# A decoder layer on one core: the last three steps of its attention in an order of their own

## The chip, the core and the metric

The kernel runs on one core of a Trainium2 chip. The number that counts is the device time of one execution in microseconds (us); the median of three runs is given. The engines are PE (matrix products and transposes), ACT, DVE and POOL (elementwise work), and SP, which here only issues DMA transfers. Each takes its instructions in the order of its own program; between engines they wait on semaphores.

## The reference

Sixteen sequences of 256 positions and 256 features pass through three parts, each with its residual added and a layer norm behind it:

```python
x = _layernorm(x + _L0_attn_ref(x, ...))            # gated mixer: projection, convolution of 4, scan, gate
x = _layernorm(x + _L0_xattn_ref(x, ctx, ctx, ...))  # cross attention, 16 heads of 16
x = _layernorm(x + _L0_ffn_ref(x, ...))              # 8 experts, one for each token
# the feed-forward part
probs = softmax(t @ Wr); idx = argmax(probs); pmax = max(probs)
pos = sum(cumsum(onehot, axis=0) * onehot, axis=-1) - 1   # place in the expert, over all 4096 tokens in order
kept = pos < 640
out = where(kept, expert_idx(t), t) * where(kept, pmax, 1)
```

The place of a token in its expert counts all tokens before it. The experts thus can't start before the last sequence has been counted.

## The kernel before

It has three blocks, with a barrier of all engines between them: `mixer_in`, `attend` and `experts`.

`attend` is a software pipeline over sequences, written once as a function `step(n, p)` for each engine. In step n, sequence n gets its keys and queries, n-1 its score maxima, n-2 and n-3 its exponentials and weighted sums, n-3 its output projection, residual and second norm, n-4 its router, counts and the scatter to `rows_dram`. `on(n, lag)` says whether sequence n-lag exists, and `run` (line 473) goes through steps -1 to 19. From step 17 on only the three last sequences are left, called X (13), Y (14) and Z (15) here. A step is laid out by 16 slots h, so what stands where is fixed by these slots, not by what is ready.

The prediction speaks of these pieces:

- PE: `scores_t` (line 756) writes a pair of heads' scores to `ps_a`, which has room for one such pair. `weigh` (766) sums the values of four heads, `sums_by_query` (782) turns the sums, `turn` (720) transposes, `project_out` (792) is the output projection, `router` (801) and `count` (809) give the logits and the running counts. All but the first two write one PSUM bank, `ps_e`; its sibling `ps_d` serves the projections of earlier sequences and has no work after step 16.
- ACT: the exponential of each pair (line 946), read from `ps_a`; copies of turned tiles to SBUF (891, 933, 951).
- DVE: the division of the sums (1063, 1064), the residual (1088), the norm that gives `pay` (999), and a chain of small operations on the router's logits: top, index, one-hot `hot` (1028), `slot0` (1030), place, `dest` (1056).
- POOL: the power -1/2 for the second norm (675) and for a third one (641), the doubled norm `twice` (645), and the scatter of `pay`, two indirect DMAs for a sequence (656).
- SP: loads. In step 16 it issues the first expert's weights, 2 MB (588, 589); after the last scatter has landed, the first expert's rows in three pieces (602).

`count` writes its counts into the columns of `ps_e` that `sums_by_query` would overwrite, so line 785 makes the sums of sequence j wait until the counts of j-1 have been read (`place_done`).

`experts` takes expert e: PE forms the hidden layer in eight parts f (line 1202, three products each of split operands). After parts 4, 5 and 6 it transposes a piece of the rows of expert e+1 (`turn_rows`, 1181, with the matmuls of line 1189), and after part 7 begins the product down (1216, 1222). SP's step (1158) loads for expert e its two weight matrices and then its rows; for e = 1 the second matrix waits for `w2_lo` of expert 0, POOL's operation of line 1357.

## Time and profile before

| | |
|---|---|
| time, median of 3 runs | 922.13 us (921.59 to 923.24) |
| the profiled execution | 924.1 us, of which the span 922.3 us |
| PE busy | 791.4 us, 86% of the span |
| DVE busy | 601.1 us, 65% |
| ACT busy | 400.9 us, 43% |
| POOL busy | 357.4 us, 39% |
| mean granted clock of PE | 0.93 of full speed |

The busy shares are averages over three blocks with different limits. Read in stretches, PE is busy 9 tenths and more of nearly every slice from 690 us to the end, and between 600 and 660 us, where attention runs out, it is not. Rows of the timeline give the start and the length of an instruction in microseconds; `xN` says how many were merged into the row, and what stands in brackets is how long the engine had been idle before it and what ended that.

### The profile page before, as it was taken

What the parts mean: (1) busy time and instruction counts of PE and PEld (TensorE: products, weight loads), DVE (VectorE), ACT (ScalarE), POOL (GpSimd) and SP (SyncE); (2) the same over time, 40 slices, a digit from 0 to 9 for tenths busy, and PEclk for the clock granted to TensorE, in tenths of its full rate; (3) what the DMA queues carried; (4) which work ended last, traced back from release to release, by engine and by line L of the source; (5) the groups of instructions that cost most, each with busy time, mean ns of one, the idle gap of its engine ahead of it and who ended that gap; (6) DMA issues with size and microseconds to landing.
All of it is one profiled execution on the core that took longest, in us unless ns stands there. A gap on an engine that the chain in (4) does not pass through costs nothing. (4 is left out here: it accounts for less than half of the span.)

```text
span 922.3 us, 16301 instructions
## 1 busy us (share of the span) xinstructions
PE 791.4 (86%) x5613; PEld 618.2 (67%) x5613; DVE 601.1 (65%) x1450; ACT 400.9 (43%) x639; POOL 357.4 (39%) x290
## 2 busy tenths in 40 slices
PE   4999873588998999999999998876389999999992
PEld 3777652355666666676666666544389999999992
DVE  4888856455578767777877777643346667666652
ACT  4666630114565555555555546451242334423320
POOL 0333334422254544544454453223312544245422
PEclk9999997778999999999999999895599999999997
DMA  4115701534543454554445344400223423343100
GB/s 127 47 32 153 211 1 52 147 109 139 144 153 113 136 150 127 157 162 129 130 133 165 119 135 139 149 22 22 96 75 120 133 99 92 110 133 125 42 29 18
DMA packets 75943, 100.87 MB, mean 109 GB/s; under 512 B 10993, under 2 KB 63386, under 8 KB 75888
## 3 DMA queue, kind: packets, MB, share of 16 engines
q1 hardware_dynamic: 72432, 92.03, 33.6%
q0 software_dynamic: 3456, 8.13, 2.5%
q8 instruction: 32, 0.52, 0.2%
q14 instruction: 23, 0.19, 0.1%
HBM read 65.47 MB, written 35.74 MB: 110 GB/s over the span
## 5 line engine op out<-in xcount | busy, mean ns | idle before, releaser
L992 DVE TENSOR_REDUCE nmax<-ps_m 128x4 f32<-128x1024 f32 x128 | 156.6, 1224 | 60.9 <-PE ps_m L752 49.9
L946 ACT ACTIVATE pt<-ps_a 128x1024 f32<-128x1024 f32 x128 | 131.4, 1026 | 98.3 <-PE ps_a L762 74.7
L1269 ACT ACTIVATE hid<-ps_h 128x640 fp32r<-128x640 f32 x64 | 45.1, 705 | 145.9 <-PE ps_h L1202 145.9
L1202 PE MATMUL ps_h<-xt,w_hi 128*128 128x320 f32 x512 | 101.8, 322 | 1.0 <-DVE xt L1284 1.0
L752 PE MATMUL ps_m<-kst,qst 48*128 48x256 f32 x512 | 67.4, 342 | 25.4 <-DVE nmax L992 21.7
L1319 DVE SCALAR_TENSOR_TENSOR hid<-ps_h,hid 128x640 fp32r<-128x640 f32 x64 | 52.8, 825 | 50.0 <-ACT hid L1269 49.7
L1369 POOL DMA_INDIRECT out_rows<-gated,token x40 | 49.9, 1246 | 88.5 <-issue 88.5
L1202 PEld LDWEIGHTS ps_h<-xt,w_hi 128*128 128x128 f32 x512 | 80.8, 193 | 4.2 <-DVE hid L1319 2.2
L629 POOL TENSOR_TENSOR half<-kq,half 128x512 fp32r<-128x512 f32 x32 | 41.7, 1302 | 105.3 <-ACT half L884 105.3
L752 PEld LDWEIGHTS ps_m<-kst,qst 48*128 48x128 f32 x512 | 40.3, 194 | 62.5 <-DVE nmax L992 32.1
L1216 PE MATMUL ps_y<-w,hid 128*128 128x512 f32 x320 | 80.1, 392 | 0.0
L166 POOL TENSOR_TENSOR gated<-xh,sgate 128x512 f32<-128x512 f32 x32 | 42.3, 1322 | 88.1 <-ACT xh L259 88.1
L354 DVE SCALAR_TENSOR_TENSOR conv<-ps_xh,taps,conv 128x510 f32<-128x510 f32 (+2 forms) x96 | 71.7, 747 | 3.4
L777 PE MATMUL ps_o<-pt,vals 128*32 128x256 f32 x1024 | 72.1, 401 | 0.0
L715 PE MATMUL ps_d<-w_out_sb,y 128*128 128x256 f32 x256 | 62.2, 388 | 11.2 <-DVE y L1040 9.8
L1216 PEld LDWEIGHTS ps_y<-w,hid 128*128 128x128 f32 x320 | 57.7, 189 | 10.3
L656 POOL DMA_INDIRECT rows_dram<-pay,dest x32 | 33.1, 1036 | 75.8 <-DVE dest L1056 66.8
L715 PEld LDWEIGHTS ps_d<-w_out_sb,y 128*128 128x128 f32 x256 | 47.3, 194 | 18.6 <-issue 11.6
L1202 PE MATMUL ps_h<-xt,w_lo 128*128 128x320 f32 x256 | 59.4, 314 | 0.0
L762 PE MATMUL ps_a<-qst,kst 49*128 49x256 f32 x512 | 53.7, 288 | 0.6 <-ACT pt L946 0.4
L1357 POOL TENSOR_TENSOR w<-gated,w 128x2048 fp32r<-128x2048 f32 x8 | 39.0, 4880 | 28.1 <-ACT w L1258 28.1
L695 PE MATMUL ps_d<-ctx,w_k_sb 128*128 128x256 f32 x128 | 39.2, 435 | 10.7 <-DMA ctx<-in_ctx_t 9.6
(170 smaller groups left out, 1596.1 us busy)
## 6 DMA issues: line engine op xcount, KB each, us to landing
halves_dram<-half SPq DMA_DIRECT2D x64, 256.0 KB, 2.5
gated<-in_w SPq DMA_DIRECT2D x16, 1024.0 KB, 5.2
kst<-halves_dram SPq DMA_DIRECT2D x64, 128.0 KB, 2.7
qst<-halves_dram SPq DMA_DIRECT2D x64, 128.0 KB, 2.9
rows_dram<-blank SPq DMA_DIRECT2D x1, 5160.0 KB, 18.9
gated<-rows_dram SPq DMA_DIRECT2D x7, 645.0 KB, 4.2
x_raw<-in_x_t SPq DMA_DIRECT2D x8, 512.0 KB, 3.7
xres<-in_x SPq DMA_DIRECT2D x16, 256.0 KB, 3.4
```

The lines of the kernel that those rows point to most:

```text
L354: op = nc.vector.scalar_tensor_tensor(out[:, :, late:S], ps[:, :, 0:S - late], taps[:, m, k:k + 1], out[:, :, late:S], ALU.mult, ALU.add)
L715: mm = pe.matmul(ps_d[:, t * D:(t + 1) * D], y[:, m, t * P:(t + 1) * P], w["out"][:, m, :], start=(m == 0), stop=(m == MH - 1), skip_group ...
L752: mm = pe.matmul(ps_m[:, side, t, :], qst[base:base + MR, p, k, t * P:(t + 1) * P], kst[base:base + MR, p, k, :], start=True, stop=True, s ...
L762: mm = pe.matmul(ps_a[:, side, t, :], kst[base:base + MR + 1, p, k, t * P:(t + 1) * P], qst[base:base + MR + 1, p, k, :], start=True, stop ...
L777: mm = pe.matmul(ps_o[VW * i:VW * (i + 1), g, :], vals[:, p, t, h, :], pt[:, h // 2 % 4, h % 2, t, :], start=(t == 0), stop=(t == KT - 1), ...
L946: nc.scalar.activation(pt[:, k % 4].rearrange("p s t q -> p (s t q)"), ps_a[:].rearrange("p s t q -> p (s t q)"), ACT.Exp).then_inc(s["exp ...
L992: nc.vector.tensor_reduce(nmax[:, q, :, :, h // 2].rearrange("p t s -> p s t"), ps_m[:], AX.X, ALU.max, negate=True).then_inc(s["max_done" ...
L1202: mm = pe.matmul(ps_h[:, f % 2, c2, 0:HC], w1[a][:, p, k, f * P:(f + 1) * P], xt[:, b, p, k, c2 * HC:(c2 + 1) * HC], start=(n == 0 and k = ...
L1216: pe.matmul(ps_y[:, (p + t) % 2, 0:2 * D], hid[:, HI, f, t * P:(t + 1) * P], w2[:, p, f].rearrange("p a d -> p (a d)"), start=(f == 0), st ...
L1269: nc.scalar.activation(hid[:, HI, f, :].rearrange("p (c n) -> p c n", c=2), ps_h[:, f % 2, :, 0:HC], ACT.Relu).then_inc(s["hid_hi"], 1)
L1319: nc.vector.scalar_tensor_tensor(hid[:, LO, f, :].rearrange("p (c n) -> p c n", c=2), ps_h[:, f % 2, :, 0:HC], 0.0, hid[:, HI, f, :].rearr ...
L1369: nc.gpsimd.indirect_dma_start(out=dram["out"], out_offset=bass.IndirectOffsetOnAxis(ap=token[:, p, t:t + 1], axis=0), in_=new[:, p, t, :] ...
```

## The change

Steps 17, 18 and 19 are no longer run through `step` on PE, ACT and DVE. The pieces of `step` become functions with the same instructions, and the three engines call them in lists written out. SP and POOL keep their steps. Four things differ in what runs:

1. The lists order some pieces otherwise than the slots did.
2. Z's turned sums, its transpose and its output projection go to `ps_d` (function `bank`), without the wait for Y's counts.
3. On POOL, from step 17 on, the power for the second norm stands ahead of the scatter; on SP the first expert's weights are issued in step 17, behind the transfer of the row of maxima, and no longer in step 16.
4. In `experts`, SP issues the rows of expert 1 at the start of the block, ahead of that expert's weights.

```diff
-    def run(eng, step):
+    def run(eng, step, end=B + 4):
...
+    X, Y, Z = B - 3, B - 2, B - 1
+
+    def bank(j):
+
+        return ps_d if isinstance(j, int) and j == Z else ps_e
...
-                if isinstance(n, int) and n == B:
+                if isinstance(n, int) and n == B + 1:
                     sp.wait_ge(s["y_done"], B)
                     sp.dma_start(c["w1_raw"], ...
...
+            def rstd2(j):
+                pool.wait_ge(s["var2_ready"], j + 1)
+                nc.gpsimd.tensor_tensor(ve2[:], ve2[:], power[:], ALU.pow).then_inc(s["rstd2"], 1)
...
+                late = isinstance(n, int) and n > B
+                if late and on(n, 3):
+                    rstd2(n - 3)
                 if on(n, 4):
...
-                if on(n, 3):
-                    j = n - 3
...
+                if on(n, 3) and not late:
+                    rstd2(n - 3)
...
                     pe.wait_ge(s["oraw_hi"], j + 1)
-                    need(pe, s["place_done"], j)
+                    if bank(j) is ps_e:
+                        need(pe, s["place_done"], j)
...
-            run(pe, step)
+            run(pe, step, B + 1)
+
+            scores_t(Y, 0, NP - 2)
+            maxima_rows(Z, 1)
...
+            scores_t(Z, 1, 7)
+            turn_x2(Y, 0)
+            weigh(Z, 1, 3)
+            router(Y)
+            sums_by_query(Z, 0)
+            sums_by_query(Z, 1)
+            count(Y)
+            turn_normed(Z)
+            project_out(Z, 0)
...
-            run(dve, step)
+            run(dve, step, B + 1)
...
+            top_of(Y)
+            hot_of(ry, Y)
+            normed(oz, Z, 0)
+            normed(oz, Z, 1)
+            picked(Y)
+            placed(Y)
+            slotted(Y, 0)
+            sent_to(Y, 0)
+            residual2(Z)
...
+            def load_rows(e, p):
+                need(sp, s["res_done"], (e - 1) * TS)
+                need(sp, s["token_done"], e - 1)
+                sp.dma_start(rows[:, p], dram["rows"][bass.ds(e * CAP, CAP), :]...
...
                 if first:
-                    return
-                need(sp, s["res_done"], (e - 1) * TS)
-                need(sp, s["token_done"], e - 1)
-                sp.dma_start(rows[:, p], dram["rows"][bass.ds(e * CAP, CAP), :]...
+                    load_rows(1, 1)
+                elif not isinstance(e, int) or e > 1:
+                    load_rows(e, p)
```

On ACT one piece moves: the copy of Y's last sums stands ahead of Z's first exponential. On DVE, besides what the diff shows, the destination of X moves ahead of the division of Y's sums.

PE in step 17, before. `pay` is X's normed input to the router, `x2t` its transpose, the `ps_a` rows are Z's scores 0 and 1, `ps_o` is the last part of Y's weighted sums:

```order
L723 MATMUL ps_e<-eye,pay 128x128 [waits m_out,x2_done]
L723 MATMUL ps_e<-eye,pay 128x128 x3
L762 MATMUL ps_a<-qst,kst 128x256 [waits exp_done,m_in]
L762 MATMUL ps_a<-qst,kst 128x256 x3
L777 MATMUL ps_o<-pt,vals 32x256 [waits exp_done]
L777 MATMUL ps_o<-pt,vals 32x256 x7
L805 MATMUL ps_e<-w_r_sb,x2t 128x8 [waits x2t_out]
L805 MATMUL ps_e<-w_r_sb,x2t 128x8 x3
L762 MATMUL ps_a<-qst,kst 128x256 [waits exp_done]
L762 MATMUL ps_a<-qst,kst 128x256 x3
L815 MATMUL ps_e<-hot,tri 128x8 [waits carry_ready,hot_ready]
```

And in the changed kernel:

```order
L734 MATMUL ps_e<-eye,pay 128x128 [waits m_out,x2_done]
L734 MATMUL ps_e<-eye,pay 128x128 x3
L788 MATMUL ps_o<-pt,vals 32x256 [waits exp_done]
L788 MATMUL ps_o<-pt,vals 32x256 x7
L817 MATMUL ps_e<-w_r_sb,x2t 128x8 [waits x2t_out]
L817 MATMUL ps_e<-w_r_sb,x2t 128x8 x3
L773 MATMUL ps_a<-qst,kst 128x256 [waits exp_done,m_in]
L773 MATMUL ps_a<-qst,kst 128x256 x3
L773 MATMUL ps_a<-qst,kst 128x256 [waits exp_done]
L773 MATMUL ps_a<-qst,kst 128x256 x3
L827 MATMUL ps_e<-hot,tri 128x8 [waits carry_ready,hot_ready]
```

Z's first scores moved from ahead of Y's weighted sums and X's router to behind both.

PE in step 18, before: Y's router, Y's counts, then Z's sums and their transpose:

```order
L805 MATMUL ps_e<-w_r_sb,x2t 128x8 [waits x2t_out]
L805 MATMUL ps_e<-w_r_sb,x2t 128x8 x3
L815 MATMUL ps_e<-hot,tri 128x8 [waits carry_ready,hot_ready]
L818 MATMUL ps_e<-carry,ones_b 128x8
L815 MATMUL ps_e<-hot,tri 128x8
L817 MATMUL ps_e<-hot,ones_b 128x8
L818 MATMUL ps_e<-carry,ones_b 128x8
L789 MATMUL ps_e<-eye,oraw 128x128 [waits place_done,oraw_hi]
L789 MATMUL ps_e<-eye,oraw 128x128 x3
L789 MATMUL ps_e<-eye,oraw 128x128 [waits on_done]
L789 MATMUL ps_e<-eye,oraw 128x128 x3
L723 MATMUL ps_e<-eye,onrm 128x128 [waits on_done]
```

And in the changed kernel:

```order
L817 MATMUL ps_e<-w_r_sb,x2t 128x8 [waits x2t_out]
L817 MATMUL ps_e<-w_r_sb,x2t 128x8 x3
L801 MATMUL ps_d<-eye,oraw 128x128 [waits oraw_hi]
L801 MATMUL ps_d<-eye,oraw 128x128 x3
L801 MATMUL ps_d<-eye,oraw 128x128 [waits on_done]
L801 MATMUL ps_d<-eye,oraw 128x128 x3
L827 MATMUL ps_e<-hot,tri 128x8 [waits carry_ready,hot_ready]
L830 MATMUL ps_e<-carry,ones_b 128x8
L827 MATMUL ps_e<-hot,tri 128x8
L829 MATMUL ps_e<-hot,ones_b 128x8
L830 MATMUL ps_e<-carry,ones_b 128x8
L734 MATMUL ps_d<-eye,onrm 128x128 [waits on_done]
```

Z's two groups of sums now stand ahead of Y's counts, in the other bank, and only the first matmul of the counts waits for `hot_ready`.

POOL in steps 18 and 19, before: `twice` and scatter of Y, the power of Z's second norm, then the power of Z's third norm:

```order
L645 TENSOR_SCALAR twice<-pay,mv,ve 128x256 [waits rstd3,setup_pe]
L645 TENSOR_SCALAR twice<-pay,mv,ve 128x256
L656 DMA rows_dram<-pay,dest 5120x258 [waits pay_ready,dest_ready,setup_pe]
L656 DMA rows_dram<-pay,dest 5120x258
L675 TENSOR_TENSOR ve<-ve,power 128x2 [waits var2_ready]
L641 TENSOR_TENSOR ve<-ve,power 128x2 [waits out_sent1,var3_ready]
L645 TENSOR_SCALAR twice<-pay,mv,ve 128x256 [waits rstd3,setup_pe]
```

And in the changed kernel:

```order
L655 TENSOR_SCALAR twice<-pay,mv,ve 128x256 [waits rstd3,setup_pe]
L655 TENSOR_SCALAR twice<-pay,mv,ve 128x256
L639 TENSOR_TENSOR ve<-ve,power 128x2 [waits var2_ready]
L669 DMA rows_dram<-pay,dest 5120x258 [waits pay_ready,dest_ready,setup_pe]
L669 DMA rows_dram<-pay,dest 5120x258
L651 TENSOR_TENSOR ve<-ve,power 128x2 [waits out_sent1,var3_ready]
L655 TENSOR_SCALAR twice<-pay,mv,ve 128x256 [waits rstd3,setup_pe]
```

The scatter of Y moved behind the power of Z's second norm, so it stands directly ahead of the third norm's work for Z.

## Rows read from the trace of the kernel before

**Rows 1.** Stretches: length, busy time of PE, PEld, DVE, ACT, POOL, granted clock, DMA.
```profile
605.50:608.90 3.40, 1.88 (x23) 1.48 (x26) 2.01 (x16) 2.03 (x8) 2.10 (x2) 1.00 0.11 35
608.90:612.30 3.40, 3.40 (x24) 1.65 (x16) 0.93 (x7) 0.96 (x1) 0.00 (x0) 0.50 0.14 47
...
684.50:700.00 15.50, 15.50 (x92) 13.67 (x91) 9.81 (x18) 4.31 (x3) 6.62 (x1) 1.00 0.37 122
```

**Rows 2.** Timeline, PE, step 17: start us, us, then the instruction and the idle time before.
```profile
602.93 0.65 PE L723 MATMUL ps_e<-eye,pay 128*128 128x128 f32 x4 [1.03 <-DVE pay L999]
603.64 0.50 PE L762 MATMUL ps_a<-qst,kst 49*128 49x256 f32 x4
604.07 1.07 PE L777 MATMUL ps_o<-pt,vals 128*32 128x256 f32 x16
605.07 1.06 PE L805 MATMUL ps_e<-w_r_sb,x2t 128*128 128x8 f32 x8
606.06 0.51 PE L762 MATMUL ps_a<-qst,kst 49*128 49x256 f32 x4
...
608.29 0.51 PE L762 MATMUL ps_a<-qst,kst 49*128 49x256 f32 x4
...
611.52 0.80 PE L762 MATMUL ps_a<-qst,kst 49*128 49x256 f32 x4
...
613.44 0.50 PE L762 MATMUL ps_a<-qst,kst 49*128 49x256 f32 x4 [0.38 <-ACT pt L946]
```

**Rows 3.** Timeline, ACT, step 17: the exponentials of scores 0 and 3 of Z.
```profile
604.18 1.02 ACT L946 ACTIVATE pt<-ps_a 128x1024 f32<-128x1024 f32 x1
...
612.36 1.02 ACT L946 ACTIVATE pt<-ps_a 128x1024 f32<-128x1024 f32 x1 [2.50 <-PE ps_a L762]
```

**Rows 4.** Timeline, PE, step 18: the router of Y and the sums of Z.
```profile
624.35 1.88 PE L805 MATMUL ps_e<-w_r_sb,x2t 128*128 128x8 f32 x8
...
628.78 1.09 PE L789 MATMUL ps_e<-eye,oraw 128*128 128x128 f32 x4 [0.50 <-DVE carry L1035]
630.68 1.11 PE L789 MATMUL ps_e<-eye,oraw 128*128 128x128 f32 x4 [0.81 <-DVE onrm L1064]
632.60 1.12 PE L723 MATMUL ps_e<-eye,onrm 128*128 128x128 f32 x4 [0.81 <-DVE onrm L1064]
```

**Rows 5.** Timeline, DVE, step 18 and the last destination.
```profile
627.83 0.16 DVE L1030 TENSOR_SCALAR slot<-expert 128x2 f32<-128x2 f32 x1
...
629.90 0.26 DVE L1063 RECIPROCAL rec<-ps_e 128x16 f32<-128x16 f32 x1 [0.80 <-PE ps_e L789]
...
648.39 0.16 DVE L1056 TENSOR_TENSOR dest<-slot,over 128x2 int32<-128x2 f32 x1
```

**Rows 6.** Timeline, POOL, steps 18 and 19.
```profile
640.33 0.73 POOL L675 TENSOR_TENSOR ve<-ve,power 128x2 f32<-128x2 f32 x1 [6.41 <-DVE ve L1094]
643.25 0.70 POOL L641 TENSOR_TENSOR ve<-ve,power 128x2 f32<-128x2 f32 x1 [2.19 <-DVE ve L1009]
644.12 2.43 POOL L645 TENSOR_SCALAR twice<-pay,mv,ve 128x256 f32<-128x256 f32 x2 [0.18 <-POOL ve L641]
649.41 1.09 POOL L656 DMA_INDIRECT rows_dram<-pay,dest  x1 [2.87 <-DVE dest L1056]
650.81 0.97 POOL L656 DMA_INDIRECT rows_dram<-pay,dest  x1 [0.30 <-issue]
```

**Rows 7.** Timeline, SP: the load of expert 1's rows.
```profile
669.47 0.57 SPq L1174 DMA_DIRECT2D gated<-rows_dram  x1
```

**Rows 8.** Timeline, PE, expert 0: rows of expert 1 turned, first product down.
```profile
676.60 0.66 PE L1189 MATMUL ps_t<-eye,gated 128*128 128x128 f32 x4 [2.60 <-DMA gated<-rows_dram]
...
684.58 2.00 PE L1216 MATMUL ps_y<-w,hid 128*128 128x512 f32 x8
```

**Rows 9.** Timeline, PE, the same two places one expert later.
```profile
707.74 0.60 PE L1189 MATMUL ps_t<-eye,gated 128*128 128x128 f32 x4
...
714.12 2.00 PE L1216 MATMUL ps_y<-w,hid 128*128 128x512 f32 x8
```

More of the change, by code:

```diff
@@ L479, in run @@
             step(i * 2 + FIRST + 1, (FIRST + 1) % 2)
-        for n in range(LAST + 1, B + 4):
+        for n in range(LAST + 1, end):
             step(n, n % 2)
+    X, Y, Z = B - 3, B - 2, B - 1
+    def bank(j):
+        return ps_d if isinstance(j, int) and j == Z else ps_e
     def on(n, lag):
@@ L788, in sums_by_query @@
                 for g in range(4):
[L789 removed]
+                    mm = pe.transpose(bank(j)[:, g * P:(g + 1) * P], oraw[:, g, t * P:(t + 1) * P], eye[:])
                 mm.then_inc(s["ot_mm"], 1)
@@ L917, in step @@
                     if h == 7 and on(n, 4):
[L918 to L924 removed]
+                        gate_sum(n - 4)
                     if h == 2 and on(n, 0):
@@ L981, in mean_var, with x2_of @@
                 chain.done(op)
+            def x2_of(i, p):
+                dve.wait_ge(s["rstd2"], i + 1)
+                need(dve, sent[p], use(i, 32, p) - 32)
+                need(dve, s["out_ready"], i - 1)
+                for t in range(KT):
+                    op = nc.vector.tensor_scalar(pay[:, p, t, 0:D], c["r2"][:, t, :], mv2[:, t, 0:1],
+                                                 ve2[:, t:t + 1], ALU.subtract, ALU.mult)
+                op.then_inc(s["x2_done"], 1)
+                nc.vector.tensor_copy(pay[:, p, :, D], c["tokens"][:, bass.ds(i * KT, KT)])
@@ new lines, in hot_of @@
+            def hot_of(rc, i):
+                dve.wait_ge(s["vo_row"], 1)
+                dve.wait_ge(s["top_out"], i + 1)
+                for t in range(KT):
+                    op = nc.vector.max_index(where[:, t, :], top[:, t, :], lg[:, t, :])
+                rc.done(op)
+                rc.done(nc.vector.tensor_copy(expert[:], where[:, :, 0]))
+                for t in range(KT):
+                    op = nc.vector.tensor_scalar(hot[:, t, :], c["kinds"][:], expert[:, t:t + 1], None, ALU.is_equal)
+                op.then_inc(s["hot_ready"], 1)
+                rc.done(nc.vector.tensor_scalar(slot0[:], expert[:], float(CAP), -1.0, ALU.mult, ALU.add))
@@ new lines, in normed @@
+            def normed(oc, j, t):
+                dve.wait_ge(s["ot_mm"], 2 * j + t + 1)
+                if t == 0:
+                    need(dve, s["ont_mm"], j)
+                o4 = bank(j)[:].rearrange("p (h w) -> p h w", w=VW)
+                oc.done(nc.vector.reciprocal(rec[:], o4[:, :, HD]))
+                nc.vector.tensor_tensor(onrm[:, t].rearrange("p (h d) -> p h d", d=HD), o4[:, :, 0:HD],
+                                        rec[:, :, None].to_broadcast([P, NH, HD]), ALU.mult
+                                        ).then_inc(s["on_done"], 1)
@@ L1015, in step @@
[L1015 to L1030 removed]
+                        top_of(n - 4)
```

279 lines of the change are left out of this document (180 added, 99 removed).

## The prediction

> **What bounds the kernel now.** I first read the page's slices: PE has 9 tenths and more in nearly all of them from 690 us to the end, at the full granted clock, as the stretch 684.5 to 700 shows (15.50 busy of 15.50) [rows 1]. So what starts the experts' dense part earlier by some microseconds ends the kernel earlier by as much. Then I read the stretches of 600 to 685 us, where the slices thin out, and for each of them the timelines of PE, DVE, ACT and POOL side by side. The reader is to see two kinds of loss there. In the end of attention no engine is full: three sequences pass one by one through a chain PE, DVE, PE, ACT, and each piece waits for the one before. In expert 0, PE waits 2.60 us for a DMA, the rows of expert 1 [rows 8], and runs slowly behind it. The changed stretches are these and no others, so the sum is made up of a part for the experts, a part for step 18 and a part for step 17.
>
> **The experts: rows of expert 1 loaded first.** In the kernel before, SP issues them at 669.47 [rows 7], behind the second weight matrix, and PE gets them at 676.60, after 2.60 us of idleness [rows 8]. The issue now comes with the start of the block. The same transfer takes 7.1 us there, from 669.47 to about 676.6, beside the weights; begun some 13 us earlier it has landed before the hidden layer begins, whatever it meets. So the wait goes: 2.60 us. PE then also goes on without the slow stretch behind the wait. From the first turned piece to the start of the product down it takes 684.58 - 676.60 = 7.98 us in expert 0 [rows 8], and 714.12 - 707.74 = 6.38 us one expert later, with the same instructions and no wait before them [rows 9]. That is 1.60 us more. Sum: 4.20 us. What could be late next is POOL's split of expert 0's second matrix, which the product down needs. The issue at 669.47 stood behind the wait for it, so it is done by then [rows 7], 11 us before PE would now come to it (684.58 - 4.20 = 680.4). From below, if PE stayed at the lower clock behind the turned rows all the same, only 2.60 is left; from above, nothing in the rows gives more than 4.2.
>
> **Step 18: Z's sums in the other bank.** Before, the chain after Y's router is: DVE's top, index and one-hot, PE's counts, DVE's reading of them, and only then Z's first sums at 628.78, released by DVE's `carry` [rows 4]. Now the sums stand directly behind the router and need 1.1 us there. The router begins at 624.35 and takes 1.88, so the sums end at about 627.3, beside DVE's chain, which ends with `slot0` at 627.83 + 0.16 = 627.99 [rows 5]. DVE can begin the division at about 628.05 where it began at 629.90 [rows 5]: 1.85 us earlier. The rest keeps its distances: second sums 0.78 after the first reciprocal (630.68 - 629.90), the transpose 1.92 after these (632.60 - 630.68) [rows 4, 5]. Y's counts stand between the second sums and this transpose on PE; they are five matmuls of 8 columns and lie inside the 0.81 us for which PE waits there anyway [rows 4]. Their readers on DVE lie between the division and Z's residual, inside a wait of several microseconds for the projection. So step 18 gives 1.85 us. If the sums had to wait for anything else of that length, it would give nothing; and more than 1.85 it can't give, as DVE's own chain then ends last.
>
> **POOL's new order.** Y's scatter, two indirect DMAs, stands now between the power of Z's second norm and the third norm of Z. The power ends at 640.33 + 0.73 = 641.06, and the third norm's began at 643.25 [rows 6]. In the rows of Z the scatter starts 0.86 us after the destination is ready (648.39 + 0.16 to 649.41) and takes 2.37 (to 650.81 + 0.97) [rows 5, 6]: 3.2 us together, so POOL is free at 644.3, 1.0 us later than it is wanted. The doubled norm behind it then ends at about 647.6 and not at 646.55 (644.12 + 2.43), while the destination of Z is ready at 648.55 (all in the old clock, from which 1.85 is to be taken). Hidden, with 0.9 us to spare. X's scatter waits now for the power of Y's second norm; the next writer of its buffer is Z's normed input, which comes behind the whole of Y's chain. So this order costs nothing.
>
> **Step 17: an order that is later at first.** Z's first scores stood at 603.64, behind the transpose of X at 602.93 [rows 2]. Now Y's weighted sums and X's router are ahead of them; the sums follow about 0.6 behind the start of that transpose, which is 0.65 long, at 603.52. The weighted sums take 1.00 of issue and the router 0.99 (604.07 to 605.07 to 606.06) [rows 2]; so Z's scores 0 start at 605.51, 1.87 us later. Then the chain of one score buffer runs: exponential 0.54 after the scores start, 1.02 long, next scores 0.06 behind it, 1.62 for each pair [rows 2, 3] (604.18 - 603.64; 613.44 - 612.36). Scores 1 come at 607.13 (606.06 before), scores 2 at 608.75 (608.29 before): 0.46 us late. Most of the delay is made up, because scores 1 waited behind the router before, and X's counts, which held scores 2, are ready 0.5 us earlier.
>
> What follows hangs on the clock. In 605.5 to 608.9 PE was busy 1.88 of 3.40 us, so idle for 1.5 in all, and in the 3.4 us behind this it ran at 0.50 of its clock, the lower of its two levels, 1.2 GHz [rows 1]: scores 3 came 3.23 us after scores 2 (611.52 - 608.29), and their exponential 0.84 after them [rows 2, 3]. At full clock the same pieces need 2.02 us (0.43 from 603.64 to 604.07, 1.00, and 0.6 for turned sums as for the transpose), and the exponential 0.54. The new order leaves PE yet less to do between 605.5 and 608.9 (three sets of scores and the counts, about 1.4 us), so I take it that the clock falls again: scores 3 and all behind them 0.46 us late. At full clock they would be 0.46 - 1.21 - 0.30 = 1.05 early. In the other direction, if the lower clock comes one stretch sooner, the first two sets of scores each lose 0.30 more: 1.06 late. I take 0.45 late, the case nearest to the row, and keep -1.05 and +1.06.
>
> The Trainium skill (TensorE: Matmul & The Clock Gate, "What's actually happening") gives the lower clock as the state behind an idle stretch. By that rule the new order, whose gaps are near 1.2 us (605.51 + 0.4 to 607.13), would keep the full clock, and the sum would be 1.5 us better. The row does not bear it out: the clock fell behind a stretch that was more than half busy.
>
> **The other edits** are put at nothing. The first expert's weights go from step 16 to 17, where the long chains of three sequences lie between them and their use; SP has them behind the small transfers that Z's scores need. What they crowded in step 16 can only come sooner, and I count no gain for it. The copy that moves on ACT goes into time in which ACT would wait for Z's later scores, and X's destination has only the scatter behind it, which waits longer now anyway.
>
> **Sum against the profiled execution:** 924.1 - 4.20 - 1.85 + 0.45 = 918.5 us (the span from 922.3 to 916.7). The profiled execution is 2.0 us above the median of the runs, 922.13; against that the same 5.6 us give **916.5 us**.
>
> **Rivals.**
> - A, the forecast: 5.6 us less, 916.5. Its own range, with step 17 up to 1.06 late and the expert part between 2.6 and 4.2, is 916.1 (step 17 on time) to 918.7.
> - B, the clock holds in step 17: 4.20 + 1.85 + 1.05 = 7.1 less, 915.0. For it: the 1.5 us of idleness come in smaller pieces. Against it: less work in the stretch. It is also what the rule of the Trainium skill gives.
> - C, the end of attention gives nothing: Y's scatter on POOL holds the third norm and thereby Z's scatter, which is the last event that the experts wait for. Its spare time is 0.9 us by the rows; if an indirect DMA takes 2 us more behind another one's descriptors, or the wait for scatters that went out late comes last, the 1.85 is gone: 4.20 less, with step 17's 0.45 on top or not, 917.9 to 918.4. For it: POOL does one thing after another, so a moved scatter holds all behind it. Against: each of these DMAs in the rows takes 1.1 us or less.
> - D, the wait in expert 0 is only exchanged, for the weights' split or the clock: 1.40 less, 920.7. For it: 7.1 us for 645 KB, beside the weights, shows that the transfers crowd. Against: 11 us of spare time.
> - E, slower than before: the clock stays at its lower level through the first expert's hidden layer, because the tail before it keeps PE even less busy. Three parts of it take 6.38 us at the upper level [rows 9], 2.1 each; at the lower one four parts would take 8.5 more. 5.6 less and 8.5 more is 2.9 more than before, 925.0. It decides from the point where more than 5.6 us of work that now runs at the upper level runs at the lower. Against it: the fall of step 17 ended with PE fully busy for 3.4 us [rows 1]; scores 4, at 613.44, are 0.50 long again, scores 3 were 0.80 [rows 2].
>
> The Trainium skill (PSUM — Partial Sum Buffer, "Engine vs sequencer instructions") has the queue of GpSimd as strictly first in, first out. This is C's ground; by the rule alone Z's third norm is late by 1.0 us, which the trace's spare time covers.
>
> **How the numbers follow.** A 0.45, B 0.22, C 0.15, D 0.09, E 0.03; 0.06 for what I don't see, half of it faster. A measurement of this kernel can tell 0.2%, 1.84 us, from no change. A, B and C are beyond that: 0.82, with a part of D and of the rest 0.88 for faster; 0.08 for within; 0.04 for slower. The range takes A, B and C whole and leaves D and E out: from B less the 0.9 by which the runs shown differ from their median, 914.1, to the far end of C with as much again, 919.4 when rounded up.
>
> **What would show it.** The timeline of PE: no idle time ahead of the turned rows of expert 1, and about 6.4 us from them to the product down. DVE's first reciprocal of Z directly behind Y's `slot0`. The granted clock of the stretch behind Z's scores 2: 0.5 says A, 1.0 says B. On POOL, Z's scatter 0.9 us after the destination is ready; a longer distance says C. The forecast is wrong if Z's destination comes less than 0.7 us or more than 3.5 us earlier than 648.39 [rows 5], or if PE idles elsewhere in expert 0.

## The result, and the profile after

| | before | after |
|---|---|---|
| time, median of 8 runs | 920.1 us (916.85 to 923.24) | 916.78 us (914.5 to 918.61) |
| the profiled execution | 924.1 us, span 922.3 us | 917.73 us, span 915.9 us |
| PE busy | 791.4 us | 791.2 us |
| mean granted clock of PE | 0.93 | 0.93 |

The changed kernel takes 0.9953 of the time of the one before (95% interval 0.9936 to 0.997), which is 4.3 us less (2.8 to 5.9). The two medians by themselves lie 3.3 us apart; differences of times below are read from the ratio and its interval unless medians are named. The forecast was 5.6 us less, 0.9939 as a ratio, inside the interval. The forecast time, 916.5 us, is 0.3 us from the median of 916.78, but that closeness is luck: it was counted down from 922.13 us, the median of three runs, and eight runs have their median at 920.1 us.

The two profiled executions differ by 6.4 us of span. Cut at instructions that both have, PE's timelines give this (us; each piece runs from its name to the next):

| from the start of | before | after | difference |
|---|---|---|---|
| the span, to X's transpose | 602.93 | 599.83 | -3.10 |
| X's transpose | 18.98 | 21.43 | +2.45 |
| Y's transpose | 2.44 | 2.85 | +0.41 |
| Y's router | 8.25 | 5.76 | -2.49 |
| the transpose of Z's normed sums, to the hidden layer of expert 0 | 30.44 | 30.45 | +0.01 |
| the hidden layer, to the first turned piece of expert 1 | 13.56 | 11.49 | -2.07 |
| the turned piece, to the product down | 7.98 | 6.38 | -1.60 |
| the product down, to the end | 237.72 | 237.71 | -0.01 |

"Step 17 took" means below the second of these pieces, from X's transpose to Y's. The first line lies in code whose order the change doesn't touch; what it is, is told further down. The rest sums to -3.3 us. Of these the last three pieces, the experts, give 3.68, and the four before them, the end of attention from X's transpose on, came out 0.38 us longer (60.49 for 60.11). So in these two traces the whole gain is that of the experts. PE's rows of the changed kernel show the experts first. These are the first row of the hidden layer, the turned piece and the product down, in the form of [rows 8]: start us, us, then the instruction.

```profile
660.32 1.41 PE L1377 MATMUL ps_h<-xt,w_hi 128*128 128x320 f32 x4 [1.01 <-DVE xt L1459]
...
671.81 0.60 PE L1364 MATMUL ps_t<-eye,gated 128*128 128x128 f32 x4
...
678.19 2.00 PE L1391 MATMUL ps_y<-w,hid 128*128 128x512 f32 x8
```

The turned piece has no bracket behind it, so PE did not wait: the 2.60 us of idleness of [rows 8] are gone. From it to the product down 6.38 us pass, to the hundredth what [rows 9] had one expert later. SP's row of the same kernel has the load at the start of the block, issued 18.2 us before PE takes the rows (before: 7.1 us, from 669.47 in [rows 7] to 676.60 in [rows 8]):

```profile
653.65 0.37 SPq L1332 DMA_DIRECT2D gated<-rows_dram  x1
```

PE in step 18, from Y's router to the projection of Z, answers to [rows 4]:

```profile
624.11 1.37 PE L817 MATMUL ps_e<-w_r_sb,x2t 128*128 128x8 f32 x8
625.33 0.63 PE L801 MATMUL ps_d<-eye,oraw 128*128 128x128 f32 x4
628.05 1.01 PE L801 MATMUL ps_d<-eye,oraw 128*128 128x128 f32 x4 [2.09 <-DVE onrm L1151]
628.86 0.21 PE L827 MATMUL ps_e<-hot,tri 128*128 128x8 bf16 x1
...
629.87 1.12 PE L734 MATMUL ps_d<-eye,onrm 128*128 128x128 f32 x4 [0.70 <-DVE onrm L1151]
```

Z's first sums stand at once behind the router, and were done well before DVE could take them. DVE, in the form of [rows 5], goes from `slot0` to the first reciprocal without a wait, then waits for the second sums; the last row is Z's destination:

```profile
627.09 0.16 DVE L1120 TENSOR_SCALAR slot<-expert 128x2 f32<-128x2 f32 x1
627.28 0.26 DVE L1150 RECIPROCAL rec<-ps_d 128x16 f32<-128x16 f32 x1
...
629.10 0.26 DVE L1150 RECIPROCAL rec<-ps_d 128x16 f32<-128x16 f32 x1 [1.10 <-PE ps_d L801]
...
645.67 0.16 DVE L1143 TENSOR_TENSOR dest<-slot,over 128x2 int32<-128x2 f32 x1
```

POOL, in the form of [rows 6]:

```profile
637.46 0.72 POOL L639 TENSOR_TENSOR ve<-ve,power 128x2 f32<-128x2 f32 x1 [11.16 <-DVE ve L1165]
638.35 1.10 POOL L669 DMA_INDIRECT rows_dram<-pay,dest  x1 [0.18 <-issue]
639.76 0.98 POOL L669 DMA_INDIRECT rows_dram<-pay,dest  x1 [0.30 <-issue]
640.73 0.77 POOL L651 TENSOR_TENSOR ve<-ve,power 128x2 f32<-128x2 f32 x1
641.67 2.43 POOL L655 TENSOR_SCALAR twice<-pay,mv,ve 128x256 f32<-128x256 f32 x2 [0.18 <-POOL ve L651]
646.69 1.10 POOL L669 DMA_INDIRECT rows_dram<-pay,dest  x1 [2.59 <-DVE dest L1143]
```

Y's scatter lies between the power and the third norm, as told. The doubled norm ends at 644.10, and POOL then waits 2.59 us for the destination of Z; the scatter of Z begins 0.86 us behind that (645.67 + 0.16 to 646.69), as before. That destination is 2.72 us earlier than the 648.39 of [rows 5], but 3.10 of that already stood at X's transpose. Step 17 is where the trace went another way. PE's rows from X's transpose to the first sums of Y, for [rows 2]:

```profile
599.83 0.66 PE L734 MATMUL ps_e<-eye,pay 128*128 128x128 f32 x4 [1.03 <-DVE pay L1085]
600.41 1.07 PE L788 MATMUL ps_o<-pt,vals 128*32 128x256 f32 x16
601.41 1.06 PE L817 MATMUL ps_e<-w_r_sb,x2t 128*128 128x8 f32 x8
602.40 0.50 PE L773 MATMUL ps_a<-qst,kst 49*128 49x256 f32 x4
604.02 0.58 PE L773 MATMUL ps_a<-qst,kst 49*128 49x256 f32 x4 [1.12 <-ACT pt L973]
...
605.72 0.79 PE L773 MATMUL ps_a<-qst,kst 49*128 49x256 f32 x4 [0.89 <-ACT pt L973]
606.44 1.93 PE L788 MATMUL ps_o<-pt,vals 128*32 128x256 f32 x16
608.31 1.12 PE L801 MATMUL ps_e<-eye,oraw 128*128 128x128 f32 x4
```

Z's scores come 1.62 us apart at first, as predicted. But the clock falls beside scores 1, earlier than before, and the stretches of the changed kernel show for how long (stretch, length, busy time of PE, PEld, DVE, ACT, POOL, granted clock, DMA):

```profile
599.80:604.30 4.50, 3.35 (x36) 2.38 (x36) 2.63 (x17) 2.35 (x5) 2.93 (x3) 1.00 0.89 297
604.30:614.50 10.20, 9.23 (x64) 4.98 (x63) 2.46 (x13) 4.66 (x8) 0.20 (x1) 0.50 0.31 103
614.50:621.30 6.80, 4.74 (x40) 2.87 (x38) 2.75 (x10) 4.05 (x5) 1.46 (x2) 1.00 0.00 0
```

PE ran at 0.50, 1.2 GHz, for 10.2 us, although it was busy for 9.23 of them. Before, the lower level lasted 3.4 us [rows 1].

### The profile page after: what moved, and what is told of

It is laid out like the page before. It is cut to its first block and busy times, and to the rows that moved or that the text cites. A ratio compares the mean times of both kernels' runs of the same rounds, so it can differ in the third digit from the quotient of the medians.

```text
span 915.9 us, 16299 instructions
## 1 busy us (share of the span) xinstructions
PE 791.2 (86%) x5613; PEld 618.6 (68%) x5613; DVE 600.8 (66%) x1450; ACT 401.2 (44%) x639; POOL 357.6 (39%) x290
## 5 line engine op out<-in xcount | busy, mean ns | idle before, releaser
L1391 PEld LDWEIGHTS ps_y<-w,hid 128*128 128x128 f32 x320 | 57.7, 189 | 10.3
L1397 PEld LDWEIGHTS ps_y<-w,hid 128*128 128x128 f32 x320 | 43.0, 190 | 4.4 <-DVE hid L1494 1.9
```

The lines of the kernel that those rows point to most:

```text
L1391: pe.matmul(ps_y[:, (p + t) % 2, 0:2 * D], hid[:, HI, f, t * P:(t + 1) * P], w2[:, p, f].rearrange("p a d -> p (a d)"), start=(f == 0), st ...
```

## The experiments

Runs 1 to 10 were each compared with the kernel before on the same chip. X, Y and Z are sequences 13, 14 and 15 throughout, and "pieces" are those of the table above.

**1. The experts' edit alone**, on the kernel before.

```diff
                 if first:
-                    return
-                need(sp, s["res_done"], (e - 1) * TS)
...
+                    load_rows(1, 1)
+                elif not isinstance(e, int) or e > 1:
+                    load_rows(e, p)
```

> The kernel before with one edit: the rows of expert 1 are issued at the start of the experts' block. My theory: this alone takes 3.7 to 4.2 us, 0.996 of the time before; from the first turned rows of expert 1 to the product down 6.4 us with no wait in front. Rival (the wait is only exchanged for another in expert 0): 0.998 or nearer to 1, and a new idle stretch of PE of 1 us or more before the product down.

Measured 918.48 us, 0.9955 (0.994 to 0.9969): 4.1 us less, against 4.20 in the forecast. PE's rows at the same place:

```profile
671.01 0.60 PE L1193 MATMUL ps_t<-eye,gated 128*128 128x128 f32 x4
...
677.39 2.00 PE L1220 MATMUL ps_y<-w,hid 128*128 128x512 f32 x8
```

No wait, and 6.38 us again. From the hidden layer to the product down the trace has 17.07 us for 21.54 before, 4.47 less. By the times this one edit brings as much as the whole change (0.9955 and 0.9953).

**2. The end of attention alone**: the changed kernel with the experts' edit undone and the weights back in step 16.

```diff
-                if isinstance(n, int) and n == B + 1:
+                if isinstance(n, int) and n == B:
                     sp.wait_ge(s["y_done"], B)
...
                 if first:
-                    load_rows(1, 1)
-                elif not isinstance(e, int) or e > 1:
-                    load_rows(e, p)
+                    return
+                load_rows(e, p)
```

> The changed kernel without the edit in the experts' block and with the first expert's weights issued in step 16 again: only the new order of the last three steps and the other bank for Z. My theory: step 18 gives 1.85 us (DVE's first reciprocal of Z right behind slot0 of Y), step 17 takes back 0.5 to 2.5 us by its late scores and the clock behind them, so the time is between 0.998 and 1.001 of before. Rival (the whole gain of step 18 reaches the end and the profile of the changed kernel had a bad clock by chance): 0.997 or less.

Measured 919.92 us, 0.9981 (0.9966 to 0.9997): 1.75 us less (0.3 to 3.1), against 1.40 (1.85 - 0.45). In its trace step 17 took 19.43 us, 0.45 more than the 18.98 before, with the short stretch at the lower clock. The wait for expert 1's rows is back, and what follows it is a surprise:

```profile
673.04 0.66 PE L1363 MATMUL ps_t<-eye,gated 128*128 128x128 f32 x4 [2.03 <-DMA gated<-rows_dram]
...
679.47 2.00 PE L1390 MATMUL ps_y<-w,hid 128*128 128x512 f32 x8
```

Behind 2.03 us of idleness PE needed 6.43 us to the product down, not 7.98. So the slow stretch behind the wait is not a sure companion of the wait. The other three traces that have the wait have the stretch too: 7.98 us before, 7.91 in its repetition, 8.00 in run 4. From X's transpose to the hidden layer this kernel took 58.60 us, 1.51 less than before.

**3. The old order of step 17** in the changed kernel.

```diff
             turn_x2(X, 1)
+            scores_t(Z, 1, 0)
             weigh(Y, 0, 3)
             router(X)
-            scores_t(Z, 1, 0)
             scores_t(Z, 1, 1)
...
-            sums_out(Y, 1, s["oraw_hi"])
             exps(Z, 0)
+            sums_out(Y, 1, s["oraw_hi"])
```

> The changed kernel with the old order of step 17 on PE and ACT: Z's first scores ahead of Y's last weighted sums and X's router. My theory: Z's chain of scores starts 1.87 us earlier, and the time is 0.5 to 2 us below the changed kernel's, 0.993 to 0.995 of before. Rival (the clock alone sets step 17, the order does nothing): the same as the changed kernel, 0.995, and from X's transpose to Y's transpose again 21 us where the clock falls and 18 where it does not.

Measured 916.91 us, 0.9943 (0.9927 to 0.9958), no different from the changed kernel. The expectation, 0.5 to 2 us below the changed kernel, can't be told from its rival by these times. The trace shows that with the old order, too, the long stretch at the lower clock came, in the second of these rows.

```profile
599.00:603.00 4.00, 2.49 (x25) 1.98 (x21) 2.03 (x16) 2.54 (x8) 2.48 (x3) 0.82 1.04 390
603.00:612.30 9.30, 9.09 (x58) 4.75 (x56) 1.74 (x8) 3.71 (x5) 0.00 (x0) 0.53 0.17 55
```

Step 17 took 21.06 us. So the new order is not what makes the stretch long. The three traces of the new order with a long stretch have 21.38 to 21.51 us, 0.32 to 0.45 more, although the fall came at other places in them. In step 18 this kernel ran wholly at the lower clock, as the one before did:

```profile
620.50 1.88 PE L817 MATMUL ps_e<-w_r_sb,x2t 128*128 128x8 f32 x8
...
626.88 1.12 PE L734 MATMUL ps_d<-eye,onrm 128*128 128x128 f32 x4 [0.69 <-DVE onrm L1151]
```

From router to transpose 6.38 us, where the kernel before takes 8.25: 1.87 us, against 1.85 in the forecast. The 2.49 of the changed kernel's own trace hold 0.6 more because its router and first sums ran partly at the upper clock (1.37 and 0.63 us for 1.88 and 1.09).

**4. The weights alone in step 17**, on the kernel before.

```diff
-                if isinstance(n, int) and n == B:
+                if isinstance(n, int) and n == B + 1:
                     sp.wait_ge(s["y_done"], B)
```

> The kernel before with one edit: the first expert's weights are issued in step 17 and not in step 16. My theory: nothing, 1.000, as nothing in step 16 waited for the transfers they crowded. Rival (the 3.1 us by which the profile of the changed kernel was ahead at the start of step 17 come from freed transfers in step 16): 0.997, with the start of step 17 some 3 us earlier and the stretch from step 15 to step 17 shorter.

Measured 922.23 us, 1.0002 (0.9986 to 1.0017): no effect that the times can tell, as put in the forecast. Its step 17 took 19.05 us, with the short stretch at the lower clock, although the weights' transfer ran through it.

**5. Y's counts ahead of Z's sums** in the changed kernel, so that the bank is new and the order is old.

```diff
             router(Y)
+            count(Y)
             sums_by_query(Z, 0)
             sums_by_query(Z, 1)
-            count(Y)
             turn_normed(Z)
...
-            normed(oz, Z, 0)
-            normed(oz, Z, 1)
             picked(Y)
...
             slotted(Y, 0)
+            normed(oz, Z, 0)
             sent_to(Y, 0)
+            normed(oz, Z, 1)
```

> The changed kernel with the old order inside step 18 (Y's counts and their readers ahead of Z's sums), Z still in the other bank and without the wait for the counts' reading. My theory: of the 1.85 us that step 18 gave, the order gives the larger part; the bank alone saves only the wait for the reading of the counts, about 0.5 us. So 1.0 to 1.4 us slower than the changed kernel, 0.996 to 0.997 of before. Rival (the bank gives it all): the same as the changed kernel, 0.995.

Measured 917.05 us, 0.9963 (0.9944 to 0.9982); the difference from the changed kernel is too small for the times. The trace has it:

```profile
621.91 1.88 PE L817 MATMUL ps_e<-w_r_sb,x2t 128*128 128x8 f32 x8
625.55 0.19 PE L827 MATMUL ps_e<-hot,tri 128*128 128x8 bf16 x1 [1.76 <-DVE hot L1118]
...
625.70 1.09 PE L801 MATMUL ps_d<-eye,oraw 128*128 128x128 f32 x4
...
629.53 1.11 PE L734 MATMUL ps_d<-eye,onrm 128*128 128x128 f32 x4 [0.81 <-DVE onrm L1151]
```

From router to transpose 7.62 us. The sums no longer wait for the reading of the counts (the 0.50 us behind `carry` in [rows 4] are gone), and that is worth 0.63 of the 8.25; the other 1.24, down to 6.38, come from the order. The bank is what permits the order, and is worth little by itself.

**6. POOL's old order** in the changed kernel.

```diff
-                late = isinstance(n, int) and n > B
+                late = False
```

> The changed kernel with POOL's old order: scatter ahead of the second norm's power. My theory: X's and Y's scatters are ready long before the powers, so the old order is hidden too and the time is the same as the changed kernel's, 0.995. Rival (the moved scatters cost something, case C of the prediction): up to 0.002 faster than the changed kernel.

Measured 916.33 us, 0.9946 (0.9921 to 0.997), as the changed kernel. From the transpose of Z's normed sums to expert 0 the two traces agree within 0.1 us. POOL's order costs nothing and brings nothing that the times or these traces show. The long stretch at the lower clock was here too, and step 17 took 21.38 us.

**7. PE kept busy in step 17.** 29 small matmuls of constants stand in PE's waits, of which nothing uses the product. They come to a bank without work there.

```diff
+            def fill(k):
+                for _ in range(k):
+                    pe.matmul(ps_m[:, 0, 0, 0:P], ones_b[:], tri[:], start=True, stop=True, skip_group_check=True)
...
             scores_t(Y, 0, NP - 1)
+            fill(10)
             turn_x2(X, 1)
...
             scores_t(Z, 1, 0)
+            fill(11)
             scores_t(Z, 1, 1)
             count(X)
+            fill(8)
             scores_t(Z, 1, 2)
```

> The changed kernel with 29 small bf16 matmuls of constants (128x128, into the score bank that is free from step 17 on) in PE's three waits of step 17: 10 ahead of X's transpose, 11 ahead of Z's scores 1, 8 ahead of scores 2. They compute nothing that is used. My theory (the clock falls because PE is idle there): the granted clock stays at 1.0 from scores 2 to scores 7 of Z and the stretch from X's transpose to Y's shrinks from 21.4 to 18 us or less; 1 to 3 us faster than the changed kernel, 0.992 to 0.994 of before. Rival (the late scores cost it, the clock is incidental): the stretch stays within 0.5 us, or grows by the fill.

Measured 913.2 us, 0.9908 (0.9878 to 0.9938), somewhat below the expected range. PE's rows show one filling and the scores around it:

```profile
603.77 0.50 PE L773 MATMUL ps_a<-qst,kst 49*128 49x256 f32 x4
604.21 0.79 PE L887 MATMUL ps_m<-tri,ones_b 128*128 128x128 bf16 x11
605.40 0.51 PE L773 MATMUL ps_a<-qst,kst 49*128 49x256 f32 x4 [0.40 <-ACT pt L980]
...
612.68 0.50 PE L773 MATMUL ps_a<-qst,kst 49*128 49x256 f32 x4
```

All scores of Z take 0.50 us, the clock did not fall, and step 17 took 17.97 us, 3.46 less than in the changed kernel. 17.97 is also 1.01 less than the 18.98 before, where rival B had 1.05. The filling costs nothing where it ends ahead of what PE waits for anyway: scores 1 follow scores 0 by 1.63 us with it and by 1.62 without.

**8. PE kept busy to the end of attention and in expert 0**: the same again in the later waits, and in `experts` fp32 products of `eye` with itself; again nothing uses them.

```diff
             scores_t(Z, 1, 7)
+            fill(18)
             turn_x2(Y, 0)
...
             sums_by_query(Z, 0)
+            fill(22)
             sums_by_query(Z, 1)
             count(Y)
+            fill(7)
             turn_normed(Z)
+            fill(6)
             project_out(Z, 0)
             project_out(Z, 1)
+            fill(42)
             turn_x2(Z, 1)
+            fill(6)
             router(Z)
+            fill(20)
             count(Z)
+            fill(70)
...
             for i in range(TURNS):
+                if i == 2:
+                    fill(12)
                 turn_rows(0, 0, i)
+            fill(4)
```

> The changed kernel with small matmuls of constants in all of PE's longer waits from step 17 to the first expert's hidden layer (29 in step 17, 121 in steps 18 and 19, 70 between the last count and the barrier, 16 of 128 columns in fp32 ahead of the first hidden part). They compute nothing that is used. My theory: the clock stays at its upper level, which shortens Z's projection (3.64 to 2.0), the routers (1.9 to 1.1), the transposes (1.1 to 0.65) and the first three hidden parts (3.2 to 1.8 each): 5 to 8 us faster than the changed kernel, 0.987 to 0.990 of before. Rival (the fill delays what is ready and the gains are hidden behind DVE and ACT): within 1.5 us of the changed kernel, or slower.

Measured 905.39 us, 0.9829 (0.9804 to 0.9854): 15.7 us less than before, the best of all, and 11.4 less than the changed kernel where 5 to 8 had been expected. The stretches, from Z's projection to the product down:

```profile
625.00:636.00 11.00, 8.20 (x108) 7.37 (x108) 6.23 (x31) 1.47 (x6) 5.94 (x6) 1.00 0.07 22
636.00:644.00 8.00, 3.26 (x59) 3.09 (x56) 0.28 (x4) 0.00 (x0) 2.06 (x2) 1.00 0.42 133
644.00:652.00 8.00, 7.70 (x51) 7.57 (x52) 3.92 (x4) 5.05 (x5) 0.10 (x1) 0.79 0.59 193
652.00:661.00 9.00, 9.00 (x63) 8.69 (x62) 3.42 (x5) 3.68 (x6) 4.64 (x1) 1.00 0.40 129
```

The full clock holds through the tail of attention and from 652 us on; the barrier's 4.9 us of idleness still cost a little at 644. The projection of Z shows one gain (the row of this kernel; in the changed kernel the same eight matmuls took 3.64 us):

```profile
624.73 1.99 PE L808 MATMUL ps_d<-w_o_sb,ont 128*128 128x256 f32 x8 [0.34 <-ACT ont L983]
```

Against the changed kernel the pieces fell by 3.46 (step 17), 1.26 (Y's transpose to router), 0.48 (to Z's normed sums), 3.10 (from these to the hidden layer) and 2.30 us (in it), 10.6 together. The spans differ by 11.9, of which 1.27 lie ahead of X's transpose, where the two kernels are alike; the medians by 11.4.

**9. The filled kernel with step 17 in its old order**, on PE and on ACT. The filling had to move with it: 17 matmuls together ahead of X's counts, in place of 11 and 8 at two places. The edit is shown against kernel 8.

```diff
+            scores_t(Z, 1, 0)
             weigh(Y, 0, 3)
             router(X)
-            scores_t(Z, 1, 0)
-            fill(11)
             scores_t(Z, 1, 1)
+            fill(17)
             count(X)
-            fill(8)
             scores_t(Z, 1, 2)
...
-            sums_out(Y, 1, s["oraw_hi"])
             exps(Z, 0)
+            sums_out(Y, 1, s["oraw_hi"])
```

> fill_all with the old order of step 17 (Z's first scores ahead of Y's weighted sums and X's router); of the fill of step 17, 17 small matmuls stand ahead of X's counts, where this order waits, and 10 ahead of X's transpose. With the clock held in both, this shows the order's own price. My theory (the new order is late by 0.46 us and nothing else): X's transpose to Y's transpose takes 17.5 us and not 17.97, and the time is that of fill_all or up to 0.5 us below it, 0.982 to 0.983 of before. Rival (with the clock held the new order is the better one): 18.2 us or more for this stretch.

Measured 905.65 us, 0.9838 (0.9814 to 0.9863), the same as 8. In the trace step 17 took 17.52 us against 17.97. So where the clock is held the new order is 0.45 us later than the old one, which is the 0.46 of the forecast by itself, and too small for the times. The two kernels differ in their filling as well, so the 0.45 is the order's only as far as each filling ended inside its wait.

**10. More filling**: kernel 8 with 60 more at the start of attention, 70 ahead of sequence 1's keys and 110, not 70, ahead of the barrier.

```diff
+            fill(60)
             run(pe, step, B + 1)
...
+                    if isinstance(j, int) and j == 1:
+                        fill(70)
...
             count(Z)
-            fill(70)
+            fill(110)
```

> fill_all with 130 more small matmuls of constants where attention starts (60 ahead of the first mixer output, 70 ahead of the second sequence's keys, where PE had waited 9.8 and 6.1 us) and 110 for 70 between the last count and the barrier. They compute nothing that is used. My theory (the same mechanism acts there): the first products of attention and the first turned rows of expert 0 run at the upper clock, and the time is 1 to 4 us below fill_all's, 0.979 to 0.982 of before. Rival (the start is bound by DMA and DVE, so the clock there costs nothing): the same as fill_all, 0.983.

Measured 908.82 us, 0.9872 (0.9846 to 0.9897), 3.4 us more than 8 by the medians, 2.2 by the spans, so neither the expectation (0.979 to 0.982) nor its rival (0.983) came true. PE's rows at the start of attention:

```profile
142.35 1.34 PE L696 MATMUL ps_d<-w_o_sb,bv_rep_sb 128*128 128x256 f32 x4 [2.56 <-PEq L120]
149.92 5.12 PE L703 MATMUL ps_m<-tri,ones_b 128*128 128x128 bf16 x60 [6.22 <-DVE ones_b L1079]
154.88 3.67 PE L732 MATMUL ps_d<-w_out_sb,y 128*128 128x256 f32 x16
```

The filling itself waited 6.22 us for one of its constants and then held the first useful product to 154.88, which came at 153.07 in kernel 8. That product ran at the full clock for it (3.67 us for 5.13), so the next one came only 0.34 us later than in kernel 8. The first row, ahead of any added filling, was already 0.60 us later (142.35 for 141.75); against that the start was 0.26 us quicker, too little to be told from chance. X's transpose came 0.63 us later. The clock fell in step 17 in spite of the filling there (0.82 in 599.2 to 606.6), which took 19.01 us for 17.97. From Z's normed sums to the hidden layer it took 0.50 us more: the larger filling at the barrier cost 0.67, and the first turned rows, which now ran at the full clock (1.07 us for 1.94), gave 0.20 back. These are the 2.2: 0.63, 1.04 and 0.50.

**11, 12. The two kernels once more**, unaltered, one execution of each, with its profile.

> The changed kernel, unaltered, for a second profile. My theory (how long the clock stays down in step 17 is chance, 3.4 us in some executions and about 9 in others, in either order): from X's transpose to Y's transpose either 19.4 or 21.4 us, and the start of step 17 anywhere between 597 and 603 us. Rival (the new order always brings the long fall): 21.4 again.

> The kernel before, unaltered, for a second profile. My theory: 19.0 us from X's transpose to Y's where the fall is short, 21.0 where it is long; from the first hidden part of expert 0 to the turned rows 13.5 us with a wait of 2 to 2.6 in front of them, and 6.4 to 8 us from there to the product down, depending on whether the clock falls in that wait. Rival (all stretches repeat to 0.1 us, so that the first profile's differences are the change's): 18.98, 13.56 and 7.98 again.

Measured 916.4 and 920.47 us (spans 914.6 and 918.7). The changed kernel had the long stretch again:

```profile
605.00:615.20 10.20, 9.81 (x60) 5.34 (x60) 1.74 (x8) 4.48 (x10) 0.00 (x0) 0.50 0.21 67
```

The kernel before had the short one again, 0.50 from 604.7 to 608.1. Its piece to X's transpose took 599.17 us, 3.76 less than in its first trace, with no change in it. Step 17, the hidden layer and the turned piece repeated the first trace, the rival's case: 18.99, 13.69 and 7.91 us for 18.98, 13.56 and 7.98. From X's transpose to the end this second pair of traces differs by 4.4 us (315.11 for 319.53), where the first differs by 3.3: the hidden layer of the changed kernel took 10.60 us this time, not 11.49.

## Why the prediction was right, and where it was not

**The experts, 4.20 us.** Right: 4.1 us by the run with this edit alone, and the wait and the load did what [rows 7, 8] promised. The split into 2.60 for the wait and 1.60 for the slow stretch is less firm than I put it. The 6.38 us came as forecast, but run 2 had them behind a wait as well, so the 1.60 depend on whether the clock falls in the wait and are not always there to be gained. And the changed kernel's first trace gives back 0.53: the hidden layer took 11.49 us to the turned piece where the kernel before took 10.96 without its wait (13.56 - 2.60), since the clock rose 5.4 us behind its start and not 3.8; in run 1 it took 10.69, in the changed kernel's second trace 10.60.

**Step 18, 1.85 us.** Right in size and place: 1.87 at the same clock (run 3, and the changed kernel's second trace, 6.38 us again). Run 5 parts it into 0.63 for the bank and 1.24 for the order. Rival C is excluded by POOL's rows and by run 6. The rule that rival C was weighed by, the strict queue of GpSimd in the Trainium skill (PSUM — Partial Sum Buffer, "Engine vs sequencer instructions"), agrees with the trace, where the third norm started at 640.73 as Y's scatter ended (639.76 + 0.98); the 2.59 us that POOL then waited for Z's destination covered it.

**POOL's scatter behind the power** was taken to need 0.86 us to start. It took 0.18, so Y's scatter held the third norm by 0.4 us (DVE's `ve` for it was ready at 640.35) and not by 1.0. Without effect on the sum.

**Step 17, 0.45 us. This is the term that was mis-sized.** The order's own price is right: 0.45 with the short stretch at the lower clock (run 2), 0.32 to 0.45 with the long one (run 3), and 0.45 with the clock held (run 9). I had bounded the clock's part by +1.06, "if the lower clock comes one stretch sooner", and took it as given that it would again last 3.4 us, because it had in [rows 1]. It lasted 10.2 us in both traces of the changed kernel, and the step took 2.45 us more, 2.0 more than forecast and 1.4 beyond the bound. The Trainium skill (TensorE: Matmul & The Clock Gate, "What's actually happening") has the upper level come back with sustained activity; here PE was busy for 9.23 and 9.81 of 10.2 us, and the upper level stayed away for all of them. It cost what attention was to bring: 2.49 us gained in step 18, 2.45 and 0.41 lost in step 17 and ahead of Y's router, so that the end of attention gave nothing in the traces of the changed kernel (60.49 and 60.46 us from X's transpose to the hidden layer, 60.11 and 60.26 before), and by the times nothing that can be told beyond run 1 (0.9953 for 0.9955). The 1.40 us that the forecast counted for it show only in run 2, where the stretch was short. Rival B's -1.05 is what the step would give with the clock held, as run 7 shows; it didn't come to pass.

Why the stretch is long in some executions stays open. It was long in four traces (after, its repetition, runs 3 and 6), all with the weights in step 17, and short in the four with the weights in step 16 and in two with the weights in step 17 (runs 4 and 5). So neither the order nor the weights' transfer decides it alone; whether this transfer makes it likelier can't be told from ten traces. Two things go with it in these traces. The fall came 4.5, 4.5, 4.6 and 5.5 us behind the start of X's transpose in the long ones, and 5.5 to 6.1 in the short ones. And in the first 3.4 us behind the fall PE was busy for 2.51, 2.52, 2.81 and 3.09 us in the long ones, for 3.19 in run 2 and for all 3.40 in the other five short ones. A fall that comes early thus meets gaps of PE that a later one doesn't, but no run moved it on purpose, so this is an observation and not a cause that is shown. That idleness of PE ahead of it brings it on is borne out by runs 7 to 9, where filling the waits kept the clock; but run 10 had a fall in spite of it, and what prolongs a fall is not shown.

**The sum.** The pieces of the two traces give 3.3 us, the times 4.3 (2.8 to 5.9), the forecast 5.6. In the traces the missing 2.3 are 2.00 in step 17, 0.41 ahead of Y's router and 0.53 in the hidden layer, where work ran at the lower clock, less 0.64 that step 18 gave beyond 1.85. The times can't part their 1.3 further. The forecast time is within 0.3 us because, by the medians, a gain 2.3 too large (5.6 for 3.3) stood against a starting value 2.0 too high. The sign that was to refute the forecast, Z's destination less than 0.7 us earlier, did not come either, and that is luck too: of the 2.72 us by which it was earlier, 3.10 arose ahead of step 17, so behind X's transpose it was 0.38 us later. Taken from there the sign says that attention's part of the forecast failed. The 0.9 us that widened the range for the spread of the runs is a rounding: the three runs lie 0.54 and 1.11 us from their median.

**Rival D** is excluded by PE's rows, which show no other wait in expert 0. **Rival E** in its form is excluded too: PE's first row of the hidden layer comes 30.45 us behind the normed sums as before, and the clock rose within the layer. What remains of it is smaller: the clock was 0.50 from the layer's start at 660.3 to 665.7, and run 8, which filled the waits ahead of it, took 2.30 us less for this piece.

## What to carry to other kernels

A load that stands in its queue behind another one's wait is the cheapest thing to move; here one moved load gave 4.1 us. A rewritten end of attention gave 1.75 alone (0.3 to 3.1), and together with the load nothing that the times can tell (0.9953 for 0.9955), as the lower clock lasted longer there. Where PE waits in short pieces, price the clock apart from the order: the same order differed by 3.5 us with the clock held or not (21.43 and 17.97), more than the 0.45 for which the order itself could be told. Small products of constants in the waits of PE's tail, most batches shorter than their wait and on operands ready long before, were worth 11.4 us here; a batch longer than its wait cost 0.67 us in run 10, and its sixty products at the start brought nothing that can be told from chance.

## What the runs showed of the hardware that was not expected

The clock can stay at its lower level through 10.2 us in which PE is busy for 9.81; elsewhere in the changed kernel it rose again behind 3.4 us (621.4 to 624.8 in its first trace, PE busy for all of them).

The kernel's time differs from execution to execution by some 3 us up and down (916.85 to 923.24 in eight runs before the change). Between the two profiled executions this shows at ACT's copies of the rows of maxima, in code that is the same. Of the changed kernel:

```profile
203.66 0.36 ACT L952 CAST mrow<-ps_e 16x256 fp32r<-16x256 f32 x1 [8.62 <-PE ps_e L751]
...
360.44 0.36 ACT L952 CAST mrow<-ps_e 16x256 fp32r<-16x256 f32 x1
```

And of the kernel before:

```profile
203.87 0.36 ACT L900 CAST mrow<-ps_e 16x256 fp32r<-16x256 f32 x1 [11.33 <-PE ps_e L740]
...
363.82 0.36 ACT L900 CAST mrow<-ps_e 16x256 fp32r<-16x256 f32 x1
```

The distance grows from 0.21 to 3.38 us between 204 and 364 us, long before the weights' load that the change moves, and is 3.10 at X's transpose. So half of the 6.4 us between the two spans is no effect of the change, and two single profiles can't be subtracted whole.

An indirect DMA on POOL began 0.18 us behind the operation ahead of it, and 0.86 us behind the end of the DVE operation that it waited for (both in the rows above).
